# The products s x z of the denominator, moved from GpSimd to VectorE

## The reference

```python
xn = layernorm(x)
q = xn @ Wq.T + bq                 # only 8 of the 32 heads are used, 128 columns each
s = elu(q) + 1                     # per head g
num = einsum('bshd,hde->bshe', s, M)
den = einsum('bshd,hd->bsh', s, z)[..., None] + 1e-6
out = repeat(num / den, 4 heads) @ Wo.T
x + out + (xn @ (w * w_scale) + b)
```

## Time and profile before

| | |
|---|---|
| median of 3 runs | 242.31 us (242.26 to 242.87) |
| the profiled execution | 243.75 us |
| its span, first to last instruction | 242.0 us |
| ScalarE busy | 119.4 us |
| GpSimd: products of z (L311) | 41.9 us in 32 operations |
| VectorE: sums (L630) | 19.4 us in 16 operations |
| granted clock of TensorE | full (2.4 GHz) in all 40 slices |
| data moved by DMA | 38.76 MB, 160 GB/s on average |

### The profile page before, as it was taken

The page is one execution under the profiler, slowest core; times in us unless marked ns, Lnnn a source line. Parts: engine busy times, 40 slices in busy tenths (PEclk is TensorE's granted clock), DMA queues, the critical chain, the costliest instruction groups (busy, mean ns, idle before and its releaser), DMA issues.

```text
span 242.0 us, 3383 instructions
## 1 busy us (share of the span) xinstructions
PE 235.2 (97%) x1030; PEld 186.9 (77%) x1030; DVE 171.5 (71%) x266; ACT 119.4 (49%) x276; POOL 101.7 (42%) x108
## 2 busy tenths in 40 slices
PE   8799999999999999999999999999999999999985
PEld 2388788886777788888888888888888888888865
DVE  2789695987998669599486794958565769853331
ACT  2655635628739824637464525355464846511110
POOL 1058734746262615245624234252405437675100
PEclk9999999999999999999999999999999999999999
DMA  7999999999391421617262727342222426876841
GB/s 215 401 416 410 395 233 214 217 212 209 100 269 20 89 56 50 172 50 165 66 196 54 193 64 158 102 119 62 89 54 76 101 78 144 185 208 148 186 175 53
DMA packets 24145, 38.76 MB, mean 160 GB/s; under 512 B 5440, under 2 KB 13376, under 8 KB 22976
## 3 DMA queue, kind: packets, MB, share of 16 engines
q1 hardware_dynamic: 19200, 26.36, 33.2%
q0 software_dynamic: 3680, 11.01, 24.0%
q10 hardware_dynamic: 1248, 1.18, 1.6%
HBM read 25.95 MB, written 4.19 MB: 125 GB/s over the span
## 4 chain that ended last, share of the span: by engine, by line
PE 87%; DVE 3%; DMA 3%; SPq 3%; ACT 1%; issue 1%; POOL 1%; DVEq 0%
PE attn_ps L790 11%; PE attn_ps L792 11%; PE attn_ps L791 11%; PE q_ps L790 10%; PE q_ps L792 10%; PE q_ps L791 10%; PE dense_ps L790 6%; PE dense_ps L792 6%; PE dense_ps L791 6%; PE attn_ps L853 3%; SPq L218 2%; DMA xT<-in_xT 2%; DMA aT<-s 1%; PE attn_ps L812 1%; PE attn_ps L824 1%
## 5 line engine op out<-in xcount | busy, mean ns | idle before, releaser
L311 POOL TENSOR_TENSOR e_and_sz<-s,z_b 128x512 f32<-128x512 f32 x32 | 41.9, 1337 | 39.1 <-DVE den L630 39.1
L438 ACT ACTIVATE s<-s,rden 128x128 f32<-128x128 f32 x128 | 39.2, 389 | 38.7 <-DVE rden L634 38.7
L790 PE MATMUL attn_ps<-P_hi,aT_hi 128*128 128x512 f32 (+1 forms) x128 | 49.8, 389 | 1.2 <-DVE aT_lo L651 1.2
L792 PE MATMUL attn_ps<-P_hi,aT_lo 128*128 128x512 f32 (+1 forms) x128 | 49.1, 384 | 0.0
L791 PE MATMUL attn_ps<-P_lo,aT_hi 128*128 128x512 f32 (+1 forms) x128 | 48.9, 382 | 0.0
L790 PE MATMUL q_ps<-WqT_hi,xT_hi 128*128 128x512 f32 x104 | 42.0, 404 | 0.3 <-DVE s L625 0.3
L792 PE MATMUL q_ps<-WqT_hi,xT_lo 128*128 128x512 f32 x104 | 40.6, 390 | 0.0
L791 PE MATMUL q_ps<-WqT_lo,xT_hi 128*128 128x512 f32 x104 | 40.5, 389 | 0.0
L286 POOL TENSOR_TENSOR xT<-xT,mean_b 128x512 f32<-128x512 f32 x13 | 18.8, 1446 | 38.7 <-ACT mean_b L387 31.4
L618 DVE SCALAR_TENSOR_TENSOR q_ps<-q_ps,rstd,bq_b 128x512 f32<-128x512 f32 x28 | 21.0, 753 | 17.8 <-PE q_ps L792 17.8
L790 PEld LDWEIGHTS attn_ps<-P_hi,aT_hi 128*128 128x128 f32 x128 | 24.0, 188 | 6.9 <-DVE aT_lo L651 1.6
(11 more groups left out here) (82 smaller groups left out, 360.7 us busy)
## 6 DMA issues: line engine op xcount, KB each, us to landing
x<-in_WoT POOLq DMA_DIRECT2D x6, 1024.0 KB, 10.6
x<-in_x SPq DMA_DIRECT2D x16, 256.0 KB, 4.9
xT<-in_xT SPq DMA_DIRECT2D x16, 256.0 KB, 5.5
x<-in_b POOLq DMA_DIRECT2D x16, 256.0 KB, 4.2
aT<-s SPq DMA_DIRECT2D x124, 32.0 KB, 1.9
out<-x SPq DMA_DIRECT2D x15, 256.0 KB, 2.6
MT<-s SPq DMA_DIRECT2D x96, 32.0 KB, 1.9
x<-in_WoT SPq DMA_DIRECT2D x2, 1024.0 KB, 13.8
```

The source lines that it names most:

```text
L311: nc.gpsimd.tensor_tensor(sz_eps[:, :, h * D // 2:(h + 1) * D // 2].rearrange("p g (j c) -> p j g c", j=2), by_quarter(sbuf_s[:, t % SRING ...
L438: last = nc.scalar.activation(a_g, a_g, ACT.Copy, scale=rden[:, t % 2, g:g + 1])
L790: nc.tensor.matmul(out, x_hi, w_hi, start=start, stop=False)
L792: return nc.tensor.matmul(out, x_lo, w_hi, start=False, stop=stop)
```

## The change

GpSimd's `times_z` is gone with its 32 calls; what stays on GpSimd keeps its order. `denominator(t)` on VectorE now begins with one multiplication of all 1024 columns, waits for its semaphore, and goes on with the sum as before. The waits that `times_z` had stand on VectorE now. `sz_ready` counts one per tile instead of two.

```diff
-            def times_z(t, h):
-                if t == 0:
-                    pool.wait_ge(z_in, 16)
-                    pool.wait_ge(eps_set, 1)
-                else:
-                    pool.wait_ge(den_ready, t)
-                pool.wait_ge(s_ready, 2 * t + h + 1)
-                nc.gpsimd.tensor_tensor(sz_eps[:, :, h * D // 2:(h + 1) * D // 2].rearrange("p g (j c) -> p j g c", j=2),
-                                        by_quarter(sbuf_s[:, t % SRING, halves(h)]), by_quarter(z_b[:, halves(h)]), ALU.mult
-                                        ).then_inc(sz_ready, 1)
...
             for t in range(LEAD, T):
-                for u in denominators_of_step(t):
-                    times_z(u, 0)
-                    times_z(u, 1)
                 add_b(t - LEAD + 1)
                 if t + 2 < T:
                     rstd_of(t + 2)
                     center(t + 2)
-            times_z(T - 1, 0)
-            times_z(T - 1, 1)
             add_b(T - LEAD + 1)
...
             def make_a(t):
                 act.wait_ge(rden_ready, t + 1)
-                act.wait_ge(sz_ready, 2 * t + 2)
+                act.wait_ge(sz_ready, t + 1)
...
             def denominator(t):
-                dve.wait_ge(sz_ready, 2 * t + 2)
+                dve.wait_ge(s_ready, 2 * t + 2)
+                if t == 0:
+                    dve.wait_ge(z_in, 16)
+                    dve.wait_ge(eps_set, 1)
+                else:
+                    dve.wait_ge(den_ready, t)
+                nc.vector.tensor_tensor(sz_eps[:, :, 0:D].rearrange("p g (j c) -> p j g c", j=4),
+                                        by_quarter(sbuf_s[:, t % SRING, :]), by_quarter(z_b[:]), ALU.mult
+                                        ).then_inc(sz_ready, 1)
+                dve.wait_ge(sz_ready, t + 1)
                 nc.vector.reduce_sum(den[:, t % 2, :], sz_eps, AX.X).then_inc(den_ready, 1)
```

More of the change, by code:

```diff
@@ L344, in _ @@
             rstd_of(5)
-            times_z(0, 0)
             add_wo(2, 0)
-            times_z(0, 1)
             add_wo(2, 1)
@@ L350, in _ @@
             rstd_of(6)
-            times_z(1, 0)
             add_wo(3, 0)
-            times_z(1, 1)
             add_wo(3, 1)
             center(6)
-            times_z(2, 0)
-            times_z(2, 1)
             rstd_of(7)
             center(7)
-            times_z(3, 0)
-            times_z(3, 1)
             add_b(0)
```

## The result

| | before | changed |
|---|---|---|
| median of 4 runs each, us | 242.59 | 245.03 |
| lowest and highest, us | 242.26, 243.15 | 244.58, 245.81 |
| profiled execution, us | 243.75 | 245.08 |
| its span, us | 242.0 | 243.3 |

The ratio is 1.0093, with a 95% interval of 1.0065 to 1.012: slower by about 2.3 us. The forecast was +0.89, 243.2, so the sign was right and the change 1.4 us too small (the rest of the distance to 245.03 is that before itself measured 242.59 here and not 242.31). The measured time lies at the upper end of the range, 245.1.

The account below looks back on a forecast made before the run. TensorE's own work plus its waits was taken as the bound, with VectorE having 70 us to spare. Loss 1.05 plus 0.50 minus gain 0.66 gave +0.89 us, 243.2 us; range 241.4 to 245.1.

Parts of the forecast that it names:

- The product: Each of 16 new VectorE products of 1024 columns takes 1.22 us, 19.5 us of added VectorE work.
- The rival with 2.67: The strided product on VectorE costs 2.67 us instead of 1.22, total about 249.5 us; chance 0.04.
- Start: Up to 58 us: first transposition and SP's first spread 2.26 us late, covered by VectorE's waits; TensorE gains 0.24.
- The 0.24 gained at P(0): xT_lo(6) ends earlier, so P(0) takes 0.86 us in the chain instead of 1.10.
- The load of x(8): Load behind SP's first spread arrives at about 71.9, VectorE asks at 71.4; zero in the sum, 0.5 in the range.
- The P stretch: 65 to 82 us: two products and a centering between the aT_lo(0) halves make P(7) late; loss 1.05 us.
- the rival in which it doesn't get in between: GpSimd's centering stays out of the aT_lo(0) pair, P(7) isn't late; total 242.1 us, chance 0.25.
- the 0.21 that was to be saved: VectorE's 0.21 us wait at 68.70 would absorb part of the 2.44 us added before aT_lo(0).
- The landing: SP's spread behind aT_lo(0) lands 2.89 us late, delaying xT_lo(9); 0 to 1.02 us for TensorE, 0.5 taken.
- the 105.40 of the forecast: New end of xT_lo(9), before at 102.51; TensorE was to want it at 104.38, so up to 1.02 us late.
- steady steps: 98 to 190 us: VectorE is busy 10.41 of 14 us, so 1.22 more fits; cost 0.
- The end: Products fill VectorE's 2.43 us wait for GpSimd, aT_lo(10) shrinks to 1.28, last spreads start sooner; gain 0.66 us.

Follow-up runs that it names:

- tiles 0 to 3: Against the kernel before, VectorE makes the products of tiles 0 to 3 only, GpSimd the rest: 245.35 us, ratio 1.0094.
- Tiles 11 to 15 alone: Against the kernel before, VectorE makes the products of tiles 11 to 15 only, GpSimd the rest: 242.31 us, ratio 0.9973.
- tiles 4 to 15: Against the kernel before, VectorE makes the products of tiles 4 to 15, GpSimd those of 0 to 3: 242.37 us, ratio 0.9968.

## Why the forecast fell short

**The product.** 1.22 us, as taken from the multiplication of two SBUF operands; den(0)'s was forecast at 2.29 (1.07 held, then 1.22) and took 2.08. The rival with 2.67 is refuted.

**Start.** xT_lo(5) and (6) fell to 0.65 and 0.69 as forecast, and xT_lo(6) ended at 56.2 against 56.4. The first spread started 1.72 late (53.05 to 54.77), 2.26 forecast. The 0.24 gained at P(0) failed to come: that piece of the chain is 1.10 in after as it was in the earlier trace rows. P(0)'s lead-in had another cause than xT_lo(6). The load of x(8), for which the range had 0.5, was in time: the statistics at 71.54 wait for nothing.

**The P stretch.** The mechanism held link for link: aT_lo(0) at 77.00 (forecast 76.78), the centering inside its first half, 2.38 for the pair, P_lo(5) until 81.77 (forecast 81.57). Holding the centering gave 1.10 of the pair's time back, which shows the price of the lock; the rival in which it doesn't get in between was wrong here. The Trainium skill (SBUF — State Buffer, Who interferes with whom) has the shared pair as a lock held for one instruction, given to whoever starts first. The 2.38 and 1.28 agree; which of two waiting engines is let in between two instructions the page doesn't say, and these rows give it to GpSimd.

The size was 1.05 and came to 1.63. Three pieces make up the 0.58. P_lo(5) ended 0.20 later than forecast. From its end to the start of P(7) (81.77 to 81.91) pass 0.14, which the sum put at nothing. And P(7), behind a stop, takes 1.10 where the earlier trace rows has 0.86 for a P without one: 0.24, the price that the prediction took off at P(0) and didn't add here. The 0.20 comes from the first spread, which was late at a place that the prediction held to be covered:

```profile
69.07 0.69 DVE L601 SCALAR_TENSOR_TENSOR s<-q_ps,e_and_sz 128x512 f32<-128x512 f32 x1 [0.18 <-DMA aT<-s]
```

VectorE waited 0.18 for its landing, so the 0.21 that was to be saved behind it came to almost nothing. This wait differs between executions: it is there in three of the profiles with den(0) to den(3) on VectorE (aT_lo(0) starts at 76.99 to 77.08) and absent in four (76.55 to 76.66), and the wait before P(7) is 1.52 here and 1.27 with the statistics moved, where this part of the kernel is the same.

**The landing.** "Between 0 and 1.02 I take 0.5": in after it was 0. b's transfer went ahead of the landing, as the prediction allowed, but the 0 doesn't show that this was why: TensorE had lost 1.21 at the mean by then and took xT_lo(9) at 106.18 only, so that even the 105.40 of the forecast would have been in time. With b beside the landing, tiles 0 to 3, it was 0.41.

**The step that failed.** The queue behind the landing was followed on VectorE to xT_lo(9) only. On the way, between the late scores of tile 7 and those of tile 8, stand den(4) with its new product and the statistics of tile 10, on whose mean TensorE's next small product hangs. The lag of 2.9 was carried past it. Den(4), at 92.82 in before, has no term in the sum: the paragraph on steady steps begins at 98 us and says that behind den in the step stands only the addition of an attention product, while a bias and the statistics of tile 10 stand there too. Priced from the rows of before, room 1.41 and TensorE's own loss 1.05, it would have been 2.89 + 1.22 - 1.41 - 1.05 = 1.65; measured 1.21. It is the dearer of the two candidates for the same stretch, and the forecast had the cheaper one. Both ends were shown: the statistics moved ahead remove the wait, and one product more at den(4) brings one of 0.6 where there was none.

**Steady steps.** Cost 0, and 0 even with a second product in six of them. Right from tile 5 on, as far as the waits show; the times leave 0.6 us of room.

**The end.** Forecast gain 0.66. SP's spread started 2.15 later (205.16 to 207.31) where TensorE was 2.85 late: 0.70 gained on it. Tiles 11 to 15 alone gave 0.65 in 12 timed runs (0.2 to 1.1).

**The sum, with measured terms:** 1.6 + 1.2 - 0.65 = 2.2, against 2.3 timed. So the forecast's 0.89 lacked 0.55 at P(7) and, net of the 0.5 booked for the landing, 0.7 at the mean. That the measured time still lies inside the range is luck: the range had its room for a slower landing, for no gain at the end and for x(8), and none of the three came. What stays open is why the landing of one and the same spread differs between executions by some tenths of a us, at 69 us and at the end.

**A better version.** With GpSimd keeping only den(0) to den(3), or only den(2) and den(3), the kernel is faster than both: 0.9968 [0.995, 0.9986] and 0.9973 [0.9956, 0.9991].

## What to carry to other kernels

When work makes an engine late, list everything that engine hands over while it is late, to every other engine, and compare each hand-over with its own room; the first one and the biggest queue behind it are not the only ones. A lag that passes through a queue of DMAs hardly shrinks (3.11 to 2.90 here), and it adds to whatever the change puts behind it. An engine with 70 us to spare can still have a stretch where 2.4 us are too much, so move the work only where the room is.

## What the runs showed of the hardware

- **A spread landed later where GpSimd's transfer of b was issued beside its end.** From the end of SP's last issue to the scores that need it: 3.6 us in tiles 0 to 3 (issues end at 100.62, scores at 104.18) with b's transfer from GpSimd at 99.28, and 3.5 in before (97.75 to 101.23) with b at 96.60; in after at most 1.7 (100.65 to 102.39, no wait) with b at 94.53; in tiles 4 to 15 at most 1.7 (97.21 to 98.95) with b at 91.08. The position of b alone wasn't varied, so its part is argued, not shown.
- **Two instructions queued on VectorE don't keep GpSimd out**, as the 2.38 rows show, but in before VectorE's subtraction waited for both of GpSimd's queued products. The two rows point opposite ways, and no run here settles what decides the turn.
- **No pause behind the new product.** Den(1) in after:

```profile
50.92 1.22 DVE L611 TENSOR_TENSOR e_and_sz<-s,z_b 128x1024 f32<-128x1024 f32 x1
52.17 1.23 DVE L615 TENSOR_REDUCE den<-e_and_sz 128x8 f32<-128x1032 f32 x1
```

The sum that waits for the product begins 0.03 us behind its end. By the drain that the Trainium skill (VectorE: DVE Perf Modes, The DRAIN you can't avoid) puts behind each operation it would be an estimated 0.95. The trace disagrees, if the drain is to come behind the end that it shows; whether the 1.22 already holds it no row tells.
